# A post-norm decoder layer: the cross-attention softmax is divided after the values instead of before them

## The reference

```python
# query x: (8,128,128), key = value = ctx_1024: (8,128,128), 16 heads of 8
Q = query @ Wq.T; K = key @ Wk.T; V = value @ Wv.T
scores = jnp.einsum('bqhd,bkhd->bhqk', Qh, Kh) / jnp.sqrt(8)
attn = jax.nn.softmax(scores, axis=-1)
out = jnp.einsum('bhqk,bkhd->bqhd', attn, Vh)
out = out.reshape(b, s, N_HEADS * HEAD_DIM)
return out @ Wo.T

x = _layernorm(x + mamba(x));  x = _layernorm(x + xattn(x, ctx));  x = _layernorm(x + ffn(x))
```

## Time and profile before

| what | before |
|---|---|
| runs of the kernel | 401.13, 405.43 and 405.34 us, median 405.34 |
| profiled execution | 400.0 us, of which span 398.0 us from first to last instruction |
| granted TensorE clock, mean | 0.912 of full speed |
| busy, share of the span | PE 79%, DVE 74%, ACT 68%, POOL 58% |
| instructions | 5603 |

### The profile page before, as it was taken

How to read it: one execution, slowest core, us unless ns; L and a number is a source line. 1 busy time by engine, 2 the same in 40 slices (tenths; PEclk the granted TensorE clock), 3 DMA queues, 4 the chain that set the end, 5 groups by cost and what they waited for, 6 DMA issues and landing times.

```text
span 398.0 us, 5603 instructions
## 1 busy us (share of the span) xinstructions
PE 312.7 (79%) x1688; PEld 191.8 (48%) x1688; DVE 293.1 (74%) x460; ACT 269.9 (68%) x684; POOL 231.6 (58%) x148
## 2 busy tenths in 40 slices
PE   4999678799678598999999999788899875069700
PEld 3443334556345364554455547534566555059700
DVE  2849938999968989999999995879677735302335
ACT  3589579998489488899999994568999961012200
POOL 7500857899747899888888851215455452600063
PEclk9999959999969699999999999999999998559955
DMA  7975231222211112233222000000000000120112
GB/s 172 314 212 202 59 106 53 85 75 105 100 57 58 54 54 105 107 107 103 102 86 80 2 1 2 0 1 0 2 2 0 3 2 0 53 68 16 45 46 66
DMA packets 16769, 26.92 MB, mean 68 GB/s; under 512 B 1964, under 2 KB 10308, under 8 KB 16740
## 3 DMA queue, kind: packets, MB, share of 16 engines
q1 hardware_dynamic: 16036, 25.46, 19.6%
q0 software_dynamic: 704, 1.10, 1.0%
HBM read 24.00 MB, written 2.56 MB: 67 GB/s over the span
## 4 chain that ended last, share of the span: by engine, by line
PE 36%; DVE 31%; ACT 11%; issue 8%; POOL 7%; DMA 4%; SPq 0%; DVEq 0%; POOLq 0%; ACTq 0%
DVE arena L1161 18%; PE bank L702 13%; PE bank L926 5%; PE bank L835 4%; PE bank L1020 3%; DVE acc L1171 3%; POOL arena L442 3%; ACT arena L664 2%; PE bank L1028 2%; PE bank L999 2%; ACT conv_in_T L591 2%; POOL dispatched_tokens L476 2%; PE bank L740 2%; POOL arena L482 2%; PE bank L945 2%
## 5 line engine op out<-in xcount | busy, mean ns | idle before, releaser
L442 POOL TENSOR_TENSOR arena<-arena,k_maskT 128x1024 f32<-128x1024 f32 x64 | 153.2, 2414 | 51.8 <-DVE arena L1161 30.1
L1161 DVE TENSOR_TENSOR_SCAN arena<-bank,arena 128x512 f32<-128x512 f32 x128 | 147.4, 1209 | 10.3 <-ACT bank L580 9.7
L702 PE MATMUL bank<-ident,arena 128*128 128x128 f32 (+1 forms) x686 | 104.0, 289 | 47.6 <-DVE arena L1161 19.5
L702 PEld LDWEIGHTS bank<-ident,arena 128*128 128x128 f32 (+1 forms) x686 | 78.9, 146 | 113.3 <-DVE arena L1161 62.8
L580 ACT ACTIVATE bank<-delta,a_neg 128x508 f32<-128x508 f32 x128 | 88.0, 691 | 16.3 <-DVE arena L1161 13.4
L835 PE MATMUL bank<-conv_in_T,ident 128*128 128x512 f32 x192 | 97.2, 617 | 0.7 <-ACT early_weights L490 0.7
L591 ACT ACTIVATE conv_in_T<-bank,c_col 128x256 f32<-128x256 f32 x192 | 80.3, 471 | 12.7 <-PE bank L702 11.7
L468 POOL TENSOR_TENSOR arena<-arena,rsum 128x1024 f32<-128x1024 f32 x16 | 30.3, 1897 | 36.9 <-DVE rsum L1260 36.9
L664 ACT ACTIVATE arena<-arena 128x128 f32<-128x128 f32 x128 | 37.7, 295 | 7.0 <-DVE arena L1255 6.9
L835 PEld LDWEIGHTS bank<-conv_in_T,ident 128*128 128x128 f32 x192 | 33.1, 199 | 19.0 <-issue 15.1
L926 PE MATMUL bank<-k_maskT,uT 128*128 128x512 f32 x64 | 30.9, 607 | 1.4 <-DVE uT L1239 0.8
(11 more groups left out here) (164 smaller groups left out, 339.3 us busy)
## 6 DMA issues: line engine op xcount, KB each, us to landing
k_maskT<-b_rows SPq DMA_DIRECT2D x32, 512.0 KB, 3.7
w_sb<-in_L_ffn_w SPq DMA_DIRECT2D x1, 2048.0 KB, 11.0
dispatched_tokens<-zeros SPq DMA_DIRECT2D x1, 640.0 KB, 15.4
expert_outputs<-arena SPq DMA_DIRECT2D x4, 160.0 KB, 2.1
x_tok<-in_x SPq DMA_DIRECT2D x1, 512.0 KB, 3.9
ctx_tok<-in_ctx SPq DMA_DIRECT2D x1, 512.0 KB, 3.9
out<-arena SPq DMA_DIRECT2D x2, 256.0 KB, 2.3
arena<-dispatched_tokens SPq DMA_DIRECT2D x1, 384.0 KB, 3.8
```

What stands on the lines that cost most here:

```text
L442: gp.tensor_tensor(dBx[g % 2][h], du[:, dr, h, :], b_bc[:, g % RING, :], ALU.mult).then_inc(dBx_ok, 1)
L702: return pe.transpose(dst, src, ident[0:src.shape[0], 0:src.shape[0]])
L1161: ve.tensor_tensor_scan(o, a, v, 0.0, ALU.mult, ALU.add).then_inc(scanned, 1)
```

## The change

The exponentials are no longer divided before they meet V. Column 8 of each head's 32 columns in `v_pad` is set to one, so that `weigh_values` yields the row sum beside the 8 values. The result in `avT` is turned back so that tokens lie on the partitions (`turn_values`, four transposes), DVE inverts the 16 sums of a token and multiplies (`normalize_values`), the 128 x 128 result is turned again (`turn_out`, ACT copies it to `oT`), and one matmul with the plain transposed Wo projects it (`project_out`). The exps of a half become one instruction of 1024 columns without `accum_out`. POOL's product, `invert_sums`, `wo_pad` and `woT` are gone. The queries are copied once without masks; the score matmuls run over the 32 rows of their group of four heads. `ROUTE0` and the calls of the routing move to earlier steps.

```diff
-    ROUTE0 = 2 * B + 3
+    ROUTE0 = 2 * B + 1
-            if i % 2 == 0 and 4 <= i < 2 * B + 4:
-                plan += [(f"av{i // 2 - 2}", 6)]
+            if i % 2 == 1 and 3 <= i < 2 * B + 3:
+                plan += [(f"av{i // 2 - 1}", 6)]
+            if i % 2 == 1 and 7 <= i < 2 * B + 7:
+                plan += [(f"wo{i // 2 - 3}", 7)]
             if i % 2 == 1 and 5 <= i < 2 * B + 5:
-                plan += [(f"wo{i // 2 - 2}", 7)]
+                plan += [(f"avq{i // 2 - 2}", 7)]
+            if i % 2 == 0 and 6 <= i < 2 * B + 6:
+                plan += [(f"oT{i // 2 - 3}", 7)]
...
-            gp.memset(v_pad[:, :, :, DH:32], 0.0).then_inc(v_zero, 1)
+            gp.memset(v_pad[:, :, :, DH + 1:32], 0.0).then_inc(v_zero, 1)
+            gp.memset(v_pad[:, :, :, DH:DH + 1], 1.0).then_inc(v_zero, 1)
             rstds(0)
-            for i in range(2 * B):
-
-                gp.wait_ge(sums_ok, i + 1)
-                gp.tensor_tensor(prob[i % 3], prob[i % 3], rsum[:, i % 3, :].unsqueeze(2).to_broadcast([P, CH, S]),
-                                 ALU.mult).then_inc(prob_ok, 1)
...
-            evacuate("qkv", qkvT[:, :, :], lambda ap: tiles(ap[:, 0:3 * D], 3))
-            evacuate("woT", woT[:, :, :], lambda ap: tiles(ap, HEADS // GH))
+            evacuate("qkv", qkvoT[:, :, :], lambda ap: tiles(ap, 4))
...
-            sc.wait_ge(q_first_ok, 1)
-            src = to_read(sc, "q0")
-            for g in range(2, HEADS // GH):
-                last = sc.activation(q_maskT[:, g, half(0)], src, ACT.Copy, scale=group_mask[:, g:g + 1])
-            was_read("q0", last)
+            evacuate("q0", qT[:, half(0)])
...
-                    for h in range(CH):
-                        last = sc.activation(prob[i % 3][:, h, :], prob[i % 3][:, h, :], ACT.Exp, scale=SCALE,
-                                             accum_out=rsum[:, i % 3, h:h + 1])
-                    last.then_inc(exp_ok, 1)
+                    sc.activation(prob[i % 3], prob[i % 3], ACT.Exp, scale=SCALE).then_inc(exp_ok, 1)
                 if 2 <= i < 2 * B + 2:
                     c = i - 2
...
+                if i % 2 == 0 and 6 <= i < 2 * B + 6:
+                    b = i // 2 - 3
+                    if b >= 2:
+                        to_read(sc, f"wo{b - 2}")
+                    evacuate(f"oT{b}", oT[b % 2], lambda ap: ap[:, 0:S])
                 if i % 2 == 0 and 4 <= i < 2 * B + 4:
                     b = i // 2 - 2
                     if b >= 2:
-                        to_read(sc, f"wo{b - 2}")
-                    evacuate(f"av{b}", outT[b % 2])
+                        to_read(sc, f"avq{b - 2}")
+                    evacuate(f"av{b}", avT[b % 2])
...
                 for g in (2 * c, 2 * c + 1):
-                    last = pe.matmul(bank[:, g, :], q_maskT[:, g, S * b:S * b + S],
-                                     k_maskT[:, b, :, :].rearrange("p j k -> p (j k)"), start=True, stop=True)
+                    in_g = slice(GH * DH * g, GH * DH * g + GH * DH)
+                    last = pe.matmul(bank[:, g, :], qT[in_g, S * b:S * b + S],
+                                     k_maskT[in_g, b, :, :].rearrange("p j k -> p (j k)"), start=True, stop=True)
                 filled(f"s{i}", last)
 
             def turn_probs(i):
-                pe.wait_ge(prob_ok, i + 1)
+                pe.wait_ge(exp_ok, i + 1)
...
+            def turn_values(b):
+                wait_read(pe, f"av{b}")
+                dst = to_fill(pe, f"avq{b}")
+                for g in range(HEADS // GH):
+                    last = turn(dst[:, S * g:S * g + S], avT[b % 2][:, S * g:S * g + S])
+                filled(f"avq{b}", last)
+
+            def turn_out(b):
+                wait_read(pe, f"avq{b}")
+                dst = to_fill(pe, f"oT{b}")
+                filled(f"oT{b}", turn(dst[:, 0:S], o_tok[b % 2]))
+
+            def project_out(b):
+                wait_read(pe, f"oT{b}")
+                dst = to_fill(pe, f"wo{b}")
+                filled(f"wo{b}", pe.matmul(dst[:, 0:D], oT[b % 2], qkvoT[:, 3, :], start=True, stop=True))
+
...
                     scores(i + 1)
+                if i % 2 == 1 and 7 <= i < 2 * B + 7:
+                    project_out(i // 2 - 3)
                 if 2 <= i < 2 * B + 2:
                     turn_probs(i - 2)
                 if 3 <= i < 2 * B + 3:
                     weigh_values(i - 3)
                 if i % 2 == 1 and 5 <= i < 2 * B + 5:
-                    b = i // 2 - 2
-                    wait_read(pe, f"av{b}")
-                    dst = to_fill(pe, f"wo{b}")
-                    for g in range(HEADS // GH):
-                        last = pe.matmul(dst[:, 0:D], outT[b % 2][:, S * g:S * g + S], woT[:, g, :],
-                                         start=(g == 0), stop=(g == HEADS // GH - 1))
-                    filled(f"wo{b}", last)
+                    turn_values(i // 2 - 2)
+                if i % 2 == 0 and 6 <= i < 2 * B + 6:
+                    turn_out(i // 2 - 3)
                 if i == ROUTE0:
                     gate_logits(0)
...
-            def invert_sums(i):
-                ve.wait_ge(exp_ok, i + 1)
-                ve.reciprocal(rsum[:, i % 3, :], rsum[:, i % 3, :]).then_inc(sums_ok, 1)
+            def normalize_values(b):
+
+                by_head = to_read(ve, f"avq{b}").rearrange("p (h e) -> p h e", h=HEADS)
+                link(ve.reciprocal(inv_sum[:, :], by_head[:, :, DH]))
+                if b >= 2:
+                    to_read(ve, f"oT{b - 2}")
+                was_read(f"avq{b}", ve.tensor_tensor(o_tok[b % 2].rearrange("p (h e) -> p h e", h=HEADS),
+                                                     by_head[:, :, 0:DH],
+                                                     inv_sum[:, :].unsqueeze(2).to_broadcast([P, HEADS, DH]), ALU.mult))
...
                     shift_scores(i)
-                if 1 <= i <= 2 * B:
-                    invert_sums(i - 1)
                 if i == 3:
-                    was_read("q1", mask_queries(1, range(HEADS // GH)))
-                if i % 2 == 0 and 6 <= i < 2 * B + 6:
+                    evacuate("q1", qT[:, half(1)])
+                if i % 2 == 1 and 7 <= i < 2 * B + 7:
                     b = i // 2 - 3
...
                     moments_of(res2, b)
-                if i == 2 * B + 1:
+                if i % 2 == 1 and 5 <= i < 2 * B + 5:
+                    normalize_values(i // 2 - 2)
+                if i == 2 * B:
                     normalize(res2, x2, 1, 0, x2_ok)
                 if i == ROUTE0:
                     evacuate("x2T0", x2T[:, half(0)])
-            choose_expert(0)
+                if i == ROUTE0 + 1:
+                    choose_expert(0)
+                if i == ROUTE0 + 3:
+                    place_tokens(0)
             normalize(res2, x2, 1, 1, x2_ok)
-            place_tokens(0)
             choose_expert(1)
             place_tokens(1)
```

More of the change, by code:

```diff
@@ L103, in decoder_layer_kernel @@
         dtT = sb("dtT", [P, 2, NH, P])
-        wo_pad = sb("wo_pad", [P, HEADS, 32])
-        qkvT = sb("qkvT", [P, 3, D])
-        woT = sb("woT", [P, HEADS // GH, D])
+        qkvoT = sb("qkvoT", [P, 4, D])
         diag_d = sb("diag_d", [P, 2, NH, P])
@@ L130, in decoder_layer_kernel @@
         rmax = sb("rmax", [P, 2, CH])
-        rsum = sb("rsum", [P, 3, CH])
+        inv_sum = sb("inv_sum", [P, HEADS])
         route = sb("route", [P, 3, B, E])
@@ L157, in decoder_layer_kernel @@
         x1T = arena[:, 9, :]
-        q_maskT = uT[:, :, :, :].rearrange("p a h t -> p (a h) t")
+        qT = uT[:, 0, 0, :]
         prob = [arena[:, c, :].rearrange("p (h k) -> p h k", h=CH) for c in range(3)]
         probT = [arena[:, 3 + c, :].rearrange("p (h k) -> p h k", h=CH) for c in range(2)]
-        outT = [arena[:, 6, BANK * c:BANK * c + BANK] for c in range(2)]
+        avT = [arena[:, 6, BANK * c:BANK * c + BANK] for c in range(2)]
+        o_tok = [arena[:, 7, S * c:S * c + S] for c in range(2)]
+        oT = [arena[:, 7, S * c:S * c + S] for c in range(2, 4)]
         res2 = arena[:, 8, :].rearrange("p (b d) -> p b d", b=B)
@@ L197, in decoder_layer_kernel @@
         var_ok, rstd_ok, x1_ok, x2_ok = sem("var_ok"), sem("rstd_ok"), sem("x1_ok"), sem("x2_ok")
-        q_first_ok = sem("q_first_ok")
-        exp_ok, sums_ok, prob_ok = sem("exp_ok"), sem("sums_ok"), sem("prob_ok")
+        exp_ok = sem("exp_ok")
         av_half = sem("av_half")
-        wo_pad_ok, v_zero = sem("wo_pad_ok"), sem("v_zero")
+        v_zero = sem("v_zero")
         gate_d, gate_exp, route_mask = sem("gate_shifted"), sem("gate_exp"), sem("route_mask")
@@ L211, in decoder_layer_kernel @@
         plan = [("xT0", 0), ("xT1", 1), ("winT", 2), ("wkT0", 3), ("xi0", 5), ("xi1", 6), ("xproj", 7), ("dtw", 2)]
-        plan += [("u0_0", 0), ("wkT1", 4), ("u0_1", 1), ("x0_0", 5), ("x0_1", 6), ("qkv", 3), ("woutT", 4), ("woT", 7)]
+        plan += [("u0_0", 0), ("wkT1", 4), ("u0_1", 1), ("x0_0", 5), ("x0_1", 6), ("qkv", 3), ("woutT", 4)]
```

(23 more changed lines are left out.)

17 lines of the change are left out of this document (7 added, 10 removed).

## The result

| what | before | after |
|---|---|---|
| runs, median (lowest to highest) | 403.53 us (399.9 to 405.71), 20 runs | 406.62 us (402.76 to 408.71), 20 runs |
| profiled execution | 400.0 us, span 398.0 | 402.76 us, span 400.8 |
| granted TensorE clock, mean | 0.912 | 0.887 |

The ratio after to before is 1.0072, 95% interval 1.0043 to 1.0102. The change makes the kernel about 0.7% slower. The forecast was 403.7 us and 1.6 us faster. The time lies inside the stated range and the change within 1%, but it goes the wrong way. That the two times lie only 2.9 us apart is luck: the forecast took its 1.6 us off the median of three runs, 405.34, and 20 runs of the same kernel have 403.53. From there the sum gives 401.9, and the measured median is 4.7 us above that.

What follows compares the result with a forecast made beforehand. A loop of waits through ACT, PE and DVE, 7.8 us per two steps, was taken to bound the attention. Projections -0.4 and the stage -1.2 gave -1.6 us off a median of 405.34: 403.7 us, range 395 to 408.

Steps and rivals of the forecast that it cites:

- The loop: Middle of the attention: a closed chain of waits through ACT, PE and DVE takes 7.8 us per two steps.
- The start: Start of the attention: without DVE's two masked copies, the first maximum starts at 259.5 instead of 261.02.
- the 0.4 of the projections: Projections ahead of the scan: the `woT` copy goes, the weights' copy is wider; 0.4 us less in sum.
- The score matmuls: Attention scores on PE: two matmuls over 32 rows in different row groups take 0.97 us, plus 0.1 for change of shape.
- Rival 2: Score matmuls do not run side by side and cost 1.7 us instead of 1.0; no change, 405.5 us; chance 0.08.
- Four turns of the loop: Attention after step 6: 4 x 7.85 us from the shift of step 6 at 280.1 to that of step 14 at 311.5.
- The tail, 16.5 us: From the last subtraction to the last moments: longer than before, from 314.0 to 330.5 us.
- Moments to the last issue: Second half's routing: 9.7 us from moments to slots, 0.9 to the first issue, then 1.4 and twice 1.27.
- the walk: Positions followed along the whole attention stage: last scatter issue near 345.0 instead of 345.88, 0.8 us earlier.
- Rival 3: TensorE's clock falls in the attention as PE waits before every `project_out`; about 13 us more, 417 us; chance 0.10.
- Rival 4: Hand-overs in the longer tail cost more, or the clock drops only there; +1 to +3 us, 405 to 408; chance 0.10.

Runs made afterwards that it cites:

- kernel 2: The changed kernel with ACT's copy into `oT` put ahead of the exp of the same even step; 401.23 us, ratio to the kernel before 0.994.
- kernel 3: The changed kernel with ACT's exp put behind all copies of the same step; 395.77 us, ratio to the kernel before 0.977.
- Kernel 1: The changed kernel with the score matmuls of even steps 8 to 14 issued twice, in PE's wait; 404.35 us, ratio to the kernel before 1.0028.
- kernel 5: The changed kernel with ACT's exp behind the copies of its step and first-half routing back at its old steps; 392.31 us, ratio to the kernel before 0.9763.
- kernel 7: The kernel before with only queries copied once unmasked and score matmuls over 32 rows in two row groups; 399.51 us, ratio 0.9923.

## Why the prediction was wrong in sign

- **The loop: right.** 7.8 us was forecast, and 7.82 is found in every pair at full clock, with the forecast pieces and with `project_out` released by ACT's copy into `oT` 2.30 us after the even subtraction's end (279.31 to 281.61; 2.33 forecast). Kernels 2 and 3 show that ACT's order closes it: with it undone the pair falls to 7.5 and then to 6.65.
- **The start: right.** From the masked copy of K to the first maximum 1.6 us are gained, 1.5 forecast (261.02 to 259.5). With the 0.4 of the projections off, PE's first scores were forecast for 257.8 and stand at 257.69, and the end of step 6's subtraction for 279.7 and stands at 279.3. That these positions fit to 0.4 us is partly luck, since other executions with the same code up to there start up to 6 us later.
- **The score matmuls: right.** Two in two row groups take 1.06 us to the start of the next matmul, 1.07 with the change of shape forecast. Rival 2 (1.7) falls.
- **"Four turns of the loop", 4 x 7.85: the step that failed.** The sum took the full clock for granted, here and in the tail. From step 6's maximum to step 14's it took 34.40 us, of which two falls of the clock cost 2 x 1.56 = 3.1. Without them the last subtraction would end at 313.0, against 313.6 forecast.
- **The tail, 16.5 us: right at a clock of 0.87, wrong here.** Kernel 1 takes 16.59 for the same instructions at that clock. In the changed kernel it is 0.71 and the tail 2.4 us longer. No run changes the waits in the tail alone, so why its clock differs is not shown.
- **Moments to the last issue: 0.8 too long.** From the last moments to the slots it is 9.5 us (9.7 forecast), and the first late issue starts 0.44 behind the start of the slots' write, not 0.9.
- Together: 344.6 by the walk, +3.1 and +2.4 by the clock, about -1.4 by the small terms, gives 348.7; 348.75 is found. The sum of the prediction is some 0.3 better than its walk, since it took -1.2 where the walk gave -0.8, in the belief that the walk was a few tenths too long; by these small terms it was.

Rival 3 named this mechanism, with the place and the wait (1.2 us forecast before each `project_out`, 1.13 found), and gave it 0.10. Its price of 13 us supposed that the clock stays down. It came down in short stretches, every second pair, and cost 5.5. Rival 4 had a part of it as well, the clock that drops only in the tail, at +1 to +3 us, and 2.4 is found there; it too had 0.10. The loss isn't peculiar to the profiled execution: the mean granted clock of the 20 runs of the changed kernel lies between 0.868 and 0.887, and that of the 45 runs of the kernel before beside the experiments between 0.900 and 0.916. The evidence that I held against it was the window from 313 to 325 of the kernel before, where PE was busy for 8.56 of 12 us at a clock of 1.00. That window speaks for one place. Here PE was busy for 6.54 of 7.82 us, a larger share, and its waits were shorter (1.13 us, against 1.28 there), and the clock fell. Neither the mean busy share nor the length of one wait foretold the clock here; I should have given the middle sizes of this rival, +1.6 us for each pair in which the clock falls, a large part of the chance, since the forecast gain of 1.6 us was just one such fall.

The Trainium skill, "TensorE: Matmul & The Clock Gate", Part 4 (PE-mode transpose), has it that the full clock doesn't engage for transposes. The trace doesn't agree: in a pair at clock 1.00 eight transposes take 0.87 us in the chain, and 1.71 at half. That the share of transposes has a part in the falls is not excluded. The fill of kernel 1 consists of ordinary matmuls, and kernels 3 and 5, which have the same transposes in a shorter pair, also have more of the others per time.

What is shown is that the falls in the pairs go away when PE's wait before `project_out` is filled or shortened, by one profile of each kernel. Why the clock falls in every second pair and not in each, and why 0.74 us of waiting in 7.17 does nothing in kernel 7 while 1.13 in 7.82 does in the changed kernel, is left open.

## What to carry to other kernels

Load per engine bounds a pipelined stage only if no closed loop runs through the hand-written orders. Look for an instruction that waits for a late result (here the exp, for the subtraction) and stands ahead of short copies that other engines want, and put it behind them: that was worth 2 to 3% here against the changed kernel, and without it the change as a whole gave a loss, though its cheaper score matmuls alone gained 0.8%. Before an edit leaves the busiest engine waiting, price a fall of its clock at the place of the wait, as a case of its own.

## What the runs showed of the hardware

- The granted clock can fall for about 3.4 us while PE is busy for 84% of a pair (6.54 of 7.82) and never idle for longer than 1.13 us at once. Each such stretch cost 1.56 us on the chain, since V and twelve transposes ran in it.
- More work on an engine can shorten a stage: two added score matmuls in a wait took the pair from 9.38 to 7.82 us.
- Two float32 matmuls of 512 columns over 32 rows each, in different row groups, take 1.06 us to the start of the next matmul (their records last 1.13) where two over 128 rows take 1.72.
- The same kernel code reaches the attention up to 6 us sooner or later (first maximum from 258.59 to 264.91 us in seven profiles), so the profiles of two kernels are compared from a common event on.
- One exp of 128x1024 takes 1.06 us where eight of 128 columns with their sums take 8 x 0.295 = 2.36.
